# Cross attention with values by query and one row of 32 rounds; window attention's head in four transfers

## The chip, the cores and the metric

The kernel runs on one core of a Trainium2 chip. The metric is device time in microseconds (us) of one execution, taken as the median of several runs. The engines are TensorE (PE; its weight loads are PEld), VectorE (DVE), ScalarE (ACT), GpSimd (POOL) and SyncE (SP), which issues all transfers here. TensorE's clock is granted at one of two levels, 1.2 and 2.4 GHz; the profile gives the mean of a stretch as a share of 2.4 GHz.

## The reference

Two decoder layers, written as six stages on x (4 sequences, 512 tokens, 512 features). The change touches two: the attention with a window of layer 1, and its cross attention, which is, in float32:

```
q = rms(x @ Wq) * gq     # 16 heads of 128, 512 queries
k = rms(ctx @ Wk) * gk ; v = ctx @ Wv      # ctx: 512 x 256
e = exp(q @ k.T / sqrt(128))
o = (e @ v) / sum(e over the keys)
x = layernorm(x + concat(o) @ Wo)
```

## The kernel before, in words

The stages run one after the other, with a barrier between them. In each, five programs (one per engine) meet through semaphores. PSUM is 8 banks of 128x512 float32; a table gives each result a bank, and PE waits (`wait_empty`) until the last result of that bank has been read. Products with the weights and the scores are made of three products of float32r halves (`split3`, lines 198 to 200: high x high, high x low, low x high). Transposes and products with the probabilities are plain float32, and each such product is two records in the profile.

**Cross attention** (`cross_attention`, L1633) treats two heads at a time: 8 rounds for each of 4 sequences, 32 in all. A round computes the attention of heads y and, interleaved, the projections of the heads x of the next round. `turns` (L1731) puts this into loops: for each sequence a loop of seven rounds, and then a round that is preceded by `start` (the next sequence's x is turned: 16 transposes on PE from a copy `x_cur`, halves by ACT and DVE) and followed by `finish` (the normalisation, on DVE). On PE a round is: scores of both heads (24 products 128x512); `values(0)`, four products with v as weights and the probabilities (keys by queries) moving, 512 columns; `queries(0)`; `sums(0)`, one product of ones with the probabilities summed by POOL over the key tiles; `values(1)`, `sums(1)`; `queries(1)`; four `keys_values`; `project_out(0)`; the transposes of k and q (L2014); `project_out(1..3)`. The values lie as features by queries, so DVE inverts a whole 128x512 tile of sums (L1925), multiplies (L1928) and hands it to ACT and DVE for the halves (L1874, L1932). Projections and transposes use three banks in turn, scores and outputs three, the values one each. The low halves of the new weights are made by POOL in one piece of 2048 columns and one of 1024 (L1792).

**Window attention** (`window_attention`, L1167) begins by loading the weights of the projection in one transfer of 1536 KB (L1304). ACT takes the high half of all of it in one instruction (L1366), POOL and DVE take the low half, two k blocks each (L1329, L1452). PE waits first for a chain of memsets on POOL (L1543), turns x, and then waits for all low halves (L1571) before the first projection. After it, a row for the bias is added (L1559).

The quoted core of the values before:

```
mm = pe.matmul(pb.ap(("o", h)), v[:, k, h * DX:(h + 1) * DX], probsT[:, h, k, :],
               start=(k == 0), stop=(k == T - 1))
```

Of the kernel before, what the change touches and what calls it, by code (L numbers as in the profile page):

```python
# [20 lines left out]
P = 128  # L21
B, S, D = 4, 512, 512
# [9 lines left out]
DX = 128  # L32
# [1134 lines left out]
def window_attention(c):  # L1167
# [12 lines left out]
    with ExitStack() as ctx:  # L1180
# [42 lines left out]
        weights, small = c.sem("s4_weights_loaded"), c.sem("s4_small_loaded")  # L1223
        bias_in, wo_in = c.sem("s4_bias_loaded"), c.sem("s4_wo_loaded")
        w_hi, w_lo_pool, w_lo_dve = c.sem("s4_w_hi_ready"), c.sem("s4_w_lo_first_half"), c.sem("s4_w_lo_second_half")
# [77 lines left out]
        def _(sp):  # L1303
            sp.dma_start(w[:, :, :], d["l1a_wqkvT"].rearrange("(k p) n -> p k n", p=P)).then_inc(weights, 16)  # L1304
# [14 lines left out]
        def _(pool):  # L1319
# [4 lines left out]
            pool.memset(ones[SB:SB + 1, :].bitcast(F32), 1.0)  # L1324
            pool.drain()
            pool.memset(kT[STK:P, :, :].bitcast(F32), 0.0).then_inc(zeros_set, 1)
            pool.drain()
            pool.wait_ge(w_hi, 1)
            pool.tensor_tensor(w_l[:, 0:2, :], w[:, 0:2, :], w_h[:, 0:2, :].bitcast(F32), ALU.subtract).then_inc(w_lo_pool, 1)  # L1329
# [28 lines left out]
        def _(act):  # L1358
# [6 lines left out]
            act.wait_ge(weights, 16)  # L1365
# [3 lines left out]
            act.activation(bias[0:1, :], braw[0:1, :], ACT.Copy)  # L1369
            act.activation(bias[SB:SB + 1, :], braw[SB:SB + 1, :], ACT.Copy).then_inc(bias_hi, 1)  # L1370
            act.wait_ge(small, 16 * 5)
            act.activation(idb[:, :], c.ident[:, :], ACT.Copy)
            act.activation(mask[:, :], maskf, ACT.Copy).then_inc(bf_ready, 1)
            act.wait_ge(tables, 1)
            act.wait_ge(q_frame, 1)

            for ph, b, *s in seq:
                if ph == "X" and b > 0:
                    turned_hi(b, s[0])
                elif ph == "Pq":  # L1380
                    t = s[0]
                    act.wait_ge(*ps.full(0, ("Pq", b, t)))
# [44 lines left out]
                elif ph == "e":  # L1427
                    h = s[0]
                    act.wait_ge(*ps.full(0, ("e", b, h)))
                    if h % 4 == 0 and b * NH + h >= NPB:  # L1430
                        act.wait_ge(*ps.full(0, ("o", *divmod((b * NH + h - NPB) // 4, NKV), 1)))
# [10 lines left out]
        def _(dve):  # L1442
# [8 lines left out]
            dve.wait_ge(w_hi, 1)  # L1451
            dve.tensor_tensor(w_l[:, 2:KD, :], w[:, 2:KD, :], w_h[:, 2:KD, :].bitcast(F32), ALU.subtract).then_inc(w_lo_dve, 1)  # L1452
# [26 lines left out]
            dve.wait_ge(bf_ready, 1)  # L1479
# [62 lines left out]
        def _(pe):  # L1542
            pe.wait_ge(zeros_set, 1)  # L1543

# [6 lines left out]
            def projected(key, b, t, lo, hi):  # L1551
                out = ps.ap(key)[:, 0:hi - lo]
                ps.wait_empty(pe, 0, key)
                for k in range(KD):
                    split3(pe, out, (c.xhi[:, k, t * P:(t + 1) * P], c.xlo[:, k, t * P:(t + 1) * P]),
                           (w_h[:, k, lo:hi], w_l[:, k, lo:hi]), k == 0, False)
                if b == 0 and t == 0:
                    pe.wait_ge(bias_lo, 1)
# [1106 lines left out]
```

## Time and profile before

| what | value |
|---|---|
| median of 3 runs | 2571.3 us (2570.89 to 2572.88) |
| the profiled execution | 2571.21 us, its span 2569.4 us |
| PE busy over the span | 2187.9 us (85%) |
| DVE, ACT, POOL busy | 1408.9, 1207.9, 909.8 us |
| window attention | about 777 to 1165 us of the span |
| cross attention | about 1165 to 2300 us |
| a transfer of 512 KB of wq, issue to landing | 4.6 us (median of 33) |
| the transfer of 1536 KB of window weights | 6.4 us |
| `RECIPROCAL` of the sums, 128x512 | 64 of 3.356 us on DVE |

The profile is one execution of the program. Its timeline gives for each instruction, or row of equal ones, the start, the duration, the engine, the line, what is written and read, and in square brackets the idle time of that engine before it and who ended it. Matmuls are pipelined: the start of one to the start of the next is the rate, the duration is longer.

### The profile page before, as it was taken

The page shows a single profiled execution, that of the slowest core. Times are in us where ns is not written, and L with a number is a line of the kernel's source. Part 1 is how long each engine was busy: PE and PEld are TensorE (multiplying, and loading weights), DVE is VectorE, ACT ScalarE, POOL GpSimd, SP SyncE. Part 2 cuts the span into 40 slices and gives each one's busy share as a digit, 9 for nine tenths or more (in the row PEclk, how much of TensorE's full clock was granted, in tenths as well). Part 3 has the DMA queues.
Part 4 walks back from the last instruction along what each step waited for, and adds up shares of the span by engine and source line. Part 5 has one row for each costly group of instructions (what it writes and reads, how often), then busy time and mean ns, then how long its engine had stood idle before and what let it go on. Part 6 is the DMA issues. An engine that isn't in the chain of part 4 may idle for free. (4 is left out here: it accounts for less than half of the span.)

```text
span 2569.4 us, 36165 instructions
## 1 busy us (share of the span) xinstructions
PE 2187.9 (85%) x12664; PEld 1555.7 (61%) x12664; DVE 1408.9 (55%) x2138; ACT 1207.9 (47%) x2272; POOL 909.8 (35%) x569
## 2 busy tenths in 40 slices
PE   5989989867895787795999999999999999967772
PEld 4555646446774665554777767777777677744340
DVE  4656666644545435542555665557556755552637
ACT  3636464534324635534555545554555555531513
POOL 3525242410003202203455455555555555530101
PEclk9999999988897999997999999999999999988886
DMA  2000000010001000003111211121111111111001
GB/s 109 1 1 1 1 1 1 1 62 1 1 1 48 1 1 1 1 1 117 36 38 49 74 49 49 49 73 33 41 49 49 49 49 49 49 37 69 1 1 65
DMA packets 62367, 84.15 MB, mean 33 GB/s; under 512 B 6132, under 2 KB 41332, under 8 KB 61752
## 3 DMA queue, kind: packets, MB, share of 16 engines
q1 hardware_dynamic: 62264, 82.76, 9.5%
q8 instruction: 67, 1.10, 0.2%
q14 instruction: 36, 0.29, 0.0%
HBM read 74.36 MB, written 4.19 MB: 31 GB/s over the span
## 5 line engine op out<-in xcount | busy, mean ns | idle before, releaser
L1925 DVE RECIPROCAL s_inv_sums<-banks 128x512 f32<-128x512 f32 x64 | 214.8, 3356 | 343.3 <-PE banks L2038 340.0
L1799 POOL TENSOR_TENSOR s_qk_rstd<-s_mean_sq,minus_half 128x8 f32<-128x8 f32 x64 | 118.7, 1854 | 502.0 <-DVE s_mean_sq L1912 502.0
L2031 PE MATMUL banks<-s_probsT,s_v 128*128 128x512 f32 x512 | 231.2, 594 | 0.0
L1862 ACT ACTIVATE s_probsT<-banks,s_minus_bound,s_qk_rstd 128x512 f32<-128x512 f32 x256 | 177.0, 782 | 92.5 <-PE banks L200 88.5
L594 DVE TENSOR_REDUCE s_neg_max<-banks 128x1 f32<-128x512 f32 x256 | 165.4, 684 | 87.9 <-PE banks L660 86.3
L543 ACT ACTIVATE s_probsT<-banks 128x512 f32<-128x512 f32 x256 | 148.7, 600 | 81.5 <-PE banks L674 79.1
L1833 ACT ACTIVATE s_squares<-banks 128x512 f32<-128x512 f32 x64 | 38.2, 597 | 288.0 <-PE banks L200 287.9
L198 PE MATMUL banks<-s_w_proj_hi,xT_hi 128*128 (+1 forms) x512 | 170.8, 334 | 2.9 <-DVE s_ctxT_lo L1973 2.9
L2031 PEld LDWEIGHTS banks<-s_probsT,s_v 128*128 128x128 f32 x512 | 97.6, 191 | 111.1 <-issue 108.5
L1792 POOL TENSOR_TENSOR s_w_proj_lo<-s_w_proj_raw,s_w_proj_hi 128x2048 f32 (+1 forms) x33 | 152.0, 4607 | 14.0 <-ACT s_w_proj_hi L1825 14.0
L1808 POOL TENSOR_TENSOR s_probs_pair_sums<-s_probsT 128x1024 f32<-128x1024 f32 x64 | 151.0, 2360 | 7.2 <-issue 7.2
L199 PE MATMUL banks<-s_w_proj_lo,xT_hi 128*128 (+1 forms) x512 | 145.7, 285 | 0.0
L200 PE MATMUL banks<-s_w_proj_hi,xT_lo 128*128 (+1 forms) x512 | 145.6, 284 | 0.0
L482 POOL TENSOR_TENSOR x_cur<-s_probsT 128x512 f32<-128x512 f32 x64 | 82.1, 1283 | 156.6 <-PE banks L692 109.9
L660 PE MATMUL banks<-s_kT,s_qT 128*128 128x512 f32 x256 | 117.8, 464 | 7.0 <-ACT s_qT L532 3.3
L198 PE MATMUL banks<-s_wqkv_hi,xT_hi 128*128 128x512 f32 (+1 forms) x256 | 92.0, 360 | 34.6 <-POOL s_wqkv_lo L464 8.8
L674 PE MATMUL banks<-s_qT,s_kT 128*128 128x512 f32 x256 | 106.3, 415 | 16.2 <-ACT s_qT L536 14.0
L198 PEld LDWEIGHTS banks<-s_w_proj_hi,xT_hi 128*128 128x128 f32 x512 | 98.9, 193 | 18.1 <-issue 18.1
L198 PE MATMUL banks<-s_w_out_hi,s_outT_hi 128*128 (+1 forms) x256 | 104.4, 408 | 5.8 <-DVE s_outT_lo L1932 5.8
L199 PEld LDWEIGHTS banks<-s_w_proj_lo,xT_hi 128*128 128x128 f32 x512 | 99.0, 193 | 14.8 <-issue 14.8
L198 PE MATMUL banks<-s_w_proj_hi,s_ctxT_hi 128*128 (+1 forms) x256 | 101.2, 395 | 6.9 <-ACT s_v L1848 6.9
L1958 DVE TENSOR_TENSOR x_all<-banks,x_all 128x512 f32 (+1 forms) x128 | 85.5, 688 | 38.1 <-PE banks L200 35.0
(409 smaller groups left out, 5896.4 us busy)
## 6 DMA issues: line engine op xcount, KB each, us to landing
s_w_proj_raw<-l1x_wq SPq DMA_DIRECT2D x33, 512.0 KB, 4.6
s_w_out_raw<-l1x_wo SPq DMA_DIRECT2D x33, 512.0 KB, 3.6
s_w_proj_raw<-l1x_wk SPq DMA_DIRECT2D x33, 256.0 KB, 4.8
s_w_proj_raw<-l1x_wv SPq DMA_DIRECT2D x33, 256.0 KB, 5.1
x_all<-x SPq DMA_DIRECT2D x4, 1024.0 KB, 12.3
s_ctxT<-ctxT SPq DMA_DIRECT2D x8, 512.0 KB, 5.7
x_cur<-x_all SPq DMA_DIRECT2D x4, 1024.0 KB, 7.7
out<-x_all SPq DMA_DIRECT2D x4, 1024.0 KB, 4.3
```

The lines of the kernel that those rows point to most:

```text
L198: pe.matmul(out, lhs[0], rhs[0], start=start, stop=False)
L199: pe.matmul(out, lhs[0], rhs[1], start=False, stop=False)
L200: return pe.matmul(out, lhs[1], rhs[0], start=False, stop=stop)
L543: act.activation(probsT[:, h % NPB, k, :], ps.ap(s), ACT.Exp).then_inc(ps.freed(s), 1)
L594: dve.tensor_reduce(nmax[:, h % 2, t, 0:1], ps.ap(s), AX.X, ALU.max, negate=True) \
L660: pe.matmul(ps.ap(s), qT[:, h % NQB, t * P:(t + 1) * P], kT[:, h % NKV, :], start=True, stop=True).then_inc(ps.filled(s), 1)
L1792: pool.tensor_tensor(out, raw, hi.bitcast(F32), ALU.subtract).then_inc(done.sem, 1)
L1799: pool.tensor_tensor(rs[:, j, :, :], ms[:, j, :, :], c.mhalf[:, 0:T * HP].rearrange("p (t h) -> p t h", h=HP), ALU.pow) \
L1808: pool.tensor_tensor(psum2[:, :, :], probsT[:, h, 0:2, :], probsT[:, h, 2:4, :], ALU.add)
L1862: act.activation(probsT[:, h, k, :], pb.ap(("e", h, k)), ACT.Exp, bias=bound[:, 0:1], scale=rs[:, 1, k, h:h + 1]).then_inc(pb.freed(("e", ...
L1925: dve.reciprocal(inv[:, h, :], pb.ap(("sum", h))).then_inc(pb.freed(("sum", h)), 1)
L2031: mm = pe.matmul(pb.ap(("o", h)), v[:, k, h * DX:(h + 1) * DX], probsT[:, h, k, :], start=(k == 0), stop=(k == T - 1))
```

## The change

In the window attention: the weights come in four transfers, ACT takes the high half block by block, POOL takes one block of the low half (k = 1) and DVE three, PE waits block by block within the first projection, and it no longer waits for the memsets at the start. The clearing of `kT` moves behind POOL's block.

In the cross attention: the loops are gone, and one list `seq` sets the order of all engines for 32 rounds. x is turned straight from `x_all`, two rounds ahead. The values now have the probabilities as weights (128x128) and v with a column of ones moving (129 columns): 16 products of 129 columns for each head, which give queries by features, with the sum in column 128. DVE inverts two sums per partition and multiplies (`M`), and PE turns the result (`OT`, 4 transposes for each head) one round later. POOL's sums, `sums` and the 128x512 reciprocals are gone. The halves of the weights are made apart for q and for k and v. Projections and transposes have two banks instead of three, the values two for each head (5 and 6) shared by both heads, `OT` one. The normalisation is made of pieces: statistics on DVE behind each output tile, the last step on ACT.

The diff, cut to its core:

```diff
-            sp.dma_start(w[:, :, :], d["l1a_wqkvT"].rearrange("(k p) n -> p k n", p=P)).then_inc(weights, 16)
+            for k in range(KD):
+                sp.dma_start(w[:, k, :], d["l1a_wqkvT"].rearrange("(k p) n -> p k n", p=P)[:, k, :]).then_inc(weights[k], 16)
...
-            pool.tensor_tensor(w_l[:, 0:2, :], w[:, 0:2, :], w_h[:, 0:2, :].bitcast(F32), ALU.subtract).then_inc(w_lo_pool, 1)
+            pool.wait_ge(w_hi, 2)
+            pool.tensor_tensor(w_l[:, 1, :], w[:, 1, :], w_h[:, 1, :].bitcast(F32), ALU.subtract).then_inc(w_lo_pool, 1)
...
-            act.activation(w_h[:, :, :], w[:, :, :], ACT.Copy).then_inc(w_hi, 1)
+            for k in range(KD):
+                act.wait_ge(weights[k], 16)
+                act.activation(w_h[:, k, :], w[:, k, :], ACT.Copy).then_inc(w_hi, 1)
...
-            pe.wait_ge(zeros_set, 1)
...
+                    if b == 0 and t == 0 and lo == 0:
+                        pe.wait_ge(*((w_lo_pool, 1) if k == 1 else (w_lo_dve, {0: 1, 2: 2, 3: 3}[k])))
...
+        for j in range(-1, N + 1):
+            now, nxt, prv, border = 0 <= j < N, j + 1 < N, 0 <= j - 1, (j + 2) % G == 0 and j + 2 < N
+            if now:
+                seq += [("E", j, 0, k) for k in range(T)]
+            if prv:
+                seq.append(("OT", j - 1, 0))
+            if nxt:
+                seq.append(("Q", j + 1, 0))
+            if prv:
+                seq.append(("OT", j - 1, 1))
+            if now:
+                seq += [("E", j, 1, k) for k in range(T)] + [("V", j, 0)]
+            if j + 2 < N:
+                seq.append(("WQ", j + 2))
...
+                seq += [("Q", j + 1, 1), ("MQ", j + 1)]
+            if now:
+                seq.append(("M", j, 0))
...
+            if border:
+                seq += [("X", (j + 2) // G, k) for k in range(KD)]
...
+            if prv:
+                seq.append(("O", j - 1, 0))
+            if nxt:
+                seq.append(("NQ", j + 1))
+            if now:
+                seq.append(("V", j, 1))
+            if nxt:
+                seq.append(("KV", j + 1, 0))
+            if now:
+                seq.append(("M", j, 1))
+            if nxt:
+                seq += [("KV", j + 1, 1), ("TQ", j + 1, 0), ("KV", j + 1, 2)]
...
+                seq += [("TQ", j + 1, 1), ("KV", j + 1, 3), ("MK", j + 1)]
...
+            if s[0] in ("Q", "KV", "TK", "TQ") or s[0] == "X" and s[2] % 2:
+                uses.append((s, na % 2, 1))
+                na += 1
+            elif s[0] in ("E", "O", "X"):
+                uses.append((s, 2 + nb % 3, 1))
+                nb += 1
+            elif s[0] == "V":
+                uses += [((*s, u), 5 + u, 1) for u in range(2)]
+            elif s[0] == "OT":
+                uses.append((s, 7, 1))
...
+                    for u in range(2):
+                        key, tt = ("V", j, h, u), slice(2 * u, 2 * u + 2)
+                        dve.wait_ge(*ps.full(0, key))
+                        out = ps.ap(key)[:, 0:2 * (DX + 1)].rearrange("p (t n) -> p t n", t=2)
+                        dve.reciprocal(inv[:, h, tt], out[:, :, DX])
+                        dve.drain()
+                        dve.tensor_tensor(o[:, h, tt, :], out[:, :, 0:DX], inv[:, h, tt].unsqueeze(2).broadcast_to([P, 2, DX]),
+                                          ALU.mult).then_inc(ps.freed(key), 1)
...
+                                mm = pe.matmul(ps.ap(key)[:, t * (DX + 1):(t + 1) * (DX + 1)], probs[:, h, k, q_tile],
+                                               v[:, k, h, :], start=(k == 0), stop=(k == T - 1))
```

`E` are scores, `Q` and `KV` projections, `TQ` and `TK` transposes, `V` values, `M` quotients, `OT` their transposes, `O` outputs, `MQ` and `MK` mean squares, `NQ` the normalised q.

On DVE, in the middle of a round of the cross attention, there stood before (the two reciprocals of the sums, then the mean squares of the next q, then the low halves of the outputs):

```order
L1925 RECIPROCAL s_inv_sums<-banks 128x512
...
L1928 TENSOR_TENSOR s_inv_sums<-banks,s_inv_sums 128x512
...
L1909 TENSOR_REDUCE s_mean_sq<-s_squares 128x8
L1912 TENSOR_SCALAR s_mean_sq<-s_mean_sq 128x8
...
L1932 TENSOR_TENSOR s_outT_lo<-s_inv_sums,s_outT_hi 128x512
...
L1919 TENSOR_TENSOR s_q<-s_q,s_qk_rstd 128x1024
```

And now, at the same place (`x_cur` holds the squares now; the first two rows are `MQ`, the next four `M` of head 0):

```order
L1948 TENSOR_REDUCE s_mean_sq<-x_cur 128x8
L1951 TENSOR_SCALAR s_mean_sq<-s_mean_sq 128x8
L1997 RECIPROCAL s_inv_sums<-banks 128x2
L1999 TENSOR_TENSOR s_out_by_query<-banks,s_inv_sums 128x256
...
L2010 TENSOR_TENSOR x_all<-banks,x_all 128x512
L1977 TENSOR_TENSOR s_q<-s_q,s_qk_rstd 128x1024
```

The mean squares stood behind the first head's quotients and now stand ahead of them; the first output tile stands between the quotients and the normalised q.

On PE, in the part from the last query projection to the second transposes of q, there stood before (`...` stands for further products of the same kind):

```order
L2038 MATMUL banks<-s_probs_sum,ones_sb 128x512
...
L198 MATMUL banks<-s_w_proj_hi,xT_hi 128x256
...
L198 MATMUL banks<-s_w_proj_hi,s_ctxT_hi 128x512
...
L198 MATMUL banks<-s_w_out_hi,s_outT_hi 128x512
...
L2014 MATMUL banks<-ident_sb,s_k 128x128 x4
```

And now:

```order
L198 MATMUL banks<-s_w_proj_hi,xT_hi 128x256
...
L198 MATMUL banks<-s_w_out_hi,s_outT_hi 128x512
...
L2096 MATMUL banks<-s_v_and_ones,s_probsT 128x129 x16
L198 MATMUL banks<-s_w_proj_hi,s_ctxT_hi 128x512
...
L2030 MATMUL banks<-ident_sb,s_q 128x128 x4
L198 MATMUL banks<-s_w_proj_hi,s_ctxT_hi 128x512
```

The second head's values moved from ahead of the queries to behind them and behind one output tile, and the transposes of q moved in between the projections of keys and values.

## Rows read from the trace of the kernel before

**Rows 1.** Busy time by engine, stretch of cross attention (PE, PEld, DVE, ACT, POOL, granted clock).

```profile
1165.00:2293.00 1128.00, 1071.45 (x5056) 804.50 (x5056) 646.20 (x670) 576.00 (x1048) 583.68 (x261) 0.98 0.15 52
```

**Rows 2.** Timeline of PE, one round: start, duration, engine, line, operation, [idle before].

```profile
1312.21 3.60 PE L2031 MATMUL banks<-s_probsT,s_v 128*128 128x512 f32 x8
...
1315.76 0.28 PE L199 MATMUL banks<-s_w_proj_lo,xT_hi 128*128 x1
...
1318.52 1.02 PE L2038 MATMUL banks<-s_probs_sum,ones_sb 128*128 128x512 f32 x2
...
1319.37 3.60 PE L2031 MATMUL banks<-s_probsT,s_v 128*128 128x512 f32 x8
...
1326.53 0.39 PE L198 MATMUL banks<-s_w_proj_hi,s_ctxT_hi 128*128 x1
...
1333.50 1.03 PE L2014 MATMUL banks<-ident_sb,s_k 128*128 128x128 f32 x8
...
1336.24 0.39 PE L199 MATMUL banks<-s_w_out_lo,s_outT_hi 128*128 x1
...
1345.56 1.88 PE L2031 MATMUL banks<-s_probsT,s_v 128*128 128x512 f32 x4
```

**Rows 3.** Timeline of ACT in the same round.

```profile
1326.73 0.60 ACT L1833 ACTIVATE s_squares<-banks 128x512 f32<-128x512 f32 x1 [3.18 <-PE banks L200]
...
1332.31 0.38 ACT L1844 ACTIVATE s_squares<-banks 128x256 f32<-128x256 f32 x1 [0.29 <-PE banks L200]
...
1332.85 0.39 ACT L1848 ACTIVATE s_v<-banks 128x256 f32<-128x256 f32 x1
```

**Rows 4.** DVE: timeline of the same round; groups by line (busy, mean ns).

```profile
1327.86 1.21 DVE L1909 TENSOR_REDUCE s_mean_sq<-s_squares 128x8 f32<-128x1024 f32 x1
...
1329.29 1.30 DVE L1932 TENSOR_TENSOR s_outT_lo<-s_inv_sums,s_outT_hi 128x512 fp32r<-128x512 f32 x2
...
L1019 DVE RECIPROCAL s_sim_inv_sums<-s_sim_sums 128x1 f32<-128x1 f32 x16 | 1.6, 149 | 0.5 <-ACT s_probs L945 0.5
...
L1520 DVE TENSOR_TENSOR x_cur<-banks,s_inv_sums 128x128 f32<-128x128 f32 x64 | 18.7, 292 | 4.8
```

**Rows 5.** Timeline of PE in the last stage: float32 products of 128 columns.

```profile
2354.17 3.84 PE L2531 MATMUL banks<-s_kkT_by_head,s_wq 128*128 128x128 f32 x32 [0.95 <-DVE s_kkT_by_head L2342]
...
2365.00 3.74 PE L2472 MATMUL banks<-s_slotsT,s_wv 128*128 128x128 f32 x32
```

**Rows 6.** Timeline at the borders of the cross attention: SP, then PE.

```profile
1166.12 0.33 SPq L1749 DMA_DIRECT2D s_gains<-l1x_gq  x1
...
1185.22 0.55 PE L198 MATMUL banks<-s_w_proj_hi,xT_hi 128*128 128x256 f32 x1 [2.94 <-DVE s_ctxT_lo L1973]
...
1212.16 3.59 PE L2031 MATMUL banks<-s_probsT,s_v 128*128 128x512 f32 x8
...
2266.76 3.60 PE L2031 MATMUL banks<-s_probsT,s_v 128*128 128x512 f32 x8
...
2300.68 1.73 PE L2484 MATMUL banks<-ident_sb,x_all 128*128 128x128 f32 x7 [7.35 <-PEq L1646]
```

**Rows 7.** PE timeline; then busy time and granted clock of three stretches.

```profile
1503.76 0.50 PE L198 MATMUL banks<-s_w_proj_hi,s_ctxT_hi 128*128 x1 [2.29 <-ACT s_v L1848]
...
1500.00:1510.00 10.00, 7.39 (x31) 5.47 (x29) 6.28 (x9) 5.31 (x16) 2.08 (x1) 0.83 0.00 0
...
1775.00:1785.00 10.00, 7.17 (x39) 5.63 (x38) 7.65 (x12) 6.70 (x18) 2.08 (x1) 1.00 0.00 0
...
2268.00:2278.00 10.00, 7.64 (x15) 3.06 (x14) 3.38 (x2) 0.00 (x0) 8.03 (x5) 0.83 0.14 52
```

**Rows 8.** Timeline of the window attention's head: POOL, PE.

```profile
788.36 4.99 POOL L1329 TENSOR_TENSOR s_wqkv_lo<-s_probsT,s_wqkv_hi 128x1536 fp32r<-128x1536 f32 x1 [6.95 <-ACT s_wqkv_hi L1366]
...
793.71 0.77 PE L198 MATMUL banks<-s_wqkv_hi,xT_hi 128*128 128x512 f32 x1 [8.72 <-POOL s_wqkv_lo L1329]
...
798.69 0.39 PE L1559 MATMUL banks<-s_bias_rows,s_ones_rows 128*128 128x512 f32 x1
```

More of the change, by code:

```diff
@@ L1364, in _ @@
                 turned_hi(0, k)
-            act.wait_ge(weights, 16)
-            act.activation(w_h[:, :, :], w[:, :, :], ACT.Copy).then_inc(w_hi, 1)
+            for k in range(KD):
+                act.wait_ge(weights[k], 16)
+                act.activation(w_h[:, k, :], w[:, k, :], ACT.Copy).then_inc(w_hi, 1)
             act.wait_ge(bias_in, 16 * 4)
             act.wait_ge(zeros_set, 1)
[L1369 to L1374, printed above, removed]
+            for row in (SB, 0):
+                act.activation(bias[row:row + 1, :], braw[row:row + 1, :], ACT.Copy).then_inc(bias_hi, 1)
             act.wait_ge(q_frame, 1)
@@ new lines, in cross_attention @@
+        seq.append(("LX", B - 1))
+        uses, na, nb = [], 0, 0
+        for s in seq:
+            if s[0] in ("Q", "KV", "TK", "TQ") or s[0] == "X" and s[2] % 2:
[8 more added lines that the diff above has]
+                uses.append((s, 7, 1))
@@ L1889, in start @@
-            def start(b):
-                c.act_x_hi(act, b, (b, b * G), pa)
-                act.wait_ge(*ctx_in.after(b, 16))
-                act.activation(c_h[:, :, :], cT[:, :, :], ACT.Copy).then_inc(ctx_hi.sem, 1)
-            turns(act, start, body, nothing)
+                        sqr.then_inc(squared["k"].sem, 1)
+                    act.activation(kk[:, t, :], kv[:, 0:NW], ACT.Copy)
+                    if j > 0 and t == 0:
+                        act.wait_ge(*ps.full(0, ("V", j - 1, 1, 1)))
@@ new lines, in _ @@
+            for ph, j, *s in seq:
+                key = (ph, j, *s)
+                if ph == "X":
+                    turned(key, lambda t: c.x[:, j * T + t, s[0] * P:(s[0] + 1) * P])
+                elif ph == "Q":
+                    i = s[0]
+                    if i == 0:
+                        pe.wait_ge(*wq_lo.after(j, 1))
+                        if j % G == 0:
+                            for k in range(KD):
+                                pe.wait_ge(*ps.released(0, ("X", j // G, k)))
+                    ps.wait_empty(pe, 0, key)
@@ L2052, in body @@
-                if x is not None:
-                    queries(0)
-                if y is not None:
-                    sums(0)
-                    values(1)
-                    sums(1)
-                if x is not None:
-                    queries(1)
-                    for t in range(T):
-                        keys_values(t)
-                if y is not None:
-                    pe.wait_ge(*wo_lo.after(y, 1))
-                    for h in range(HP):
-                        pe.wait_ge(*pb.released(y, ("o", h)))
-                    project_out(0)
@@ L2068, in body @@
-                if x is not None:
-                    transposed("kT", kk, pa.released(x, ("kv", T - 1)))
-                    transposed("qT", q, q_normed.after(x[1], 1))
-                if y is not None:
-                    for t in range(1, T):
-                        project_out(t)
-            def start(b):
-                c.pe_turn_x(pe, b, (b, b * G), pa)
-            turns(pe, start, body, nothing)
-        pa.close(B * G, B)
-        pb.close(B * G)
-        c.close_common()
+                                        (side(wx_h, j)[:, w], side(wx_l, j)[:, w]), k == 0, k == KD - 1)
```

628 lines of the change are left out of this document (331 added, 297 removed).

## Prediction

> **What bounds the kernel now.** I read the busy times by stretch first. In the cross attention PE is busy 1071 of 1128 us, the granted clock 0.98 of 2.4 GHz [rows 1]; DVE, ACT and POOL each do about half. So PE sets the time here, and the reciprocals of 3.36 us on DVE and the sums on POOL, which the change removes, lie beside PE's work. What is to be priced is PE's own work and its waits. Then I read one round in PE's timeline [rows 2]: the values of head 0 start at 1312.21 and again at 1345.56, a round is 33.35 us. In it PE waits once, about 0.5 us, at the transposes. From the first values to those of the last round are 31 rounds, 1212.16 to 2266.76 [rows 6], 1054.6 us. At 33.35 they would be 1033.9: 20.7 us are extra, at the three changes of sequence and behind them (one is the wait of 2.29 us in [rows 7]).
>
> **Values.** Before: 1312.21 to 1315.64 (0.12, one product of 256 columns, ahead of the second one at 1315.76), 3.43 us a head; the sums take 1318.52 to 1319.37, 0.85 [rows 2]. Both heads: 8.56. Now each head has 16 products of 129 columns, 32 records. The nearest row is a chain of 16 float32 products of 128 columns, each with weights of its own: 32 records in 3.74 us, the last one lasting about 0.28, so 0.112 each [rows 5]. Ends: 0.112, and 0.118 from the other row (3.84 us, with a slow first one). I take 0.112, whose operands are alike in form: 3.6 us a head, 7.2 both (7.6 at 0.118).
>
> **Transposes.** Before: 1333.50 to 1336.01 (0.23 ahead of 1336.24), 2.51 with the wait, for 16 [rows 2]. Now 24, in six groups of four, each between float32r products. Eight in a row take 0.87; a group of four and the way back to float32r about 0.50, against 0.44 from that rate alone. I take 0.50: 3.0 in all (2.6 at the lower end). The other products, 33.35 - 8.56 - 2.51 = 22.3, stay as they are. Work of a round: 22.3 + 7.2 + 3.0 = 32.5.
>
> **First new wait: the second head's values.** On PE the order is the second query projection, one output tile (6 products of 0.23, 1.38 us), then the values of head 1. These need bank 5, which held the first head's values and is freed by the quotient `M` on DVE. But `M` stands on DVE behind the mean squares `MQ` of the projection that PE has just ended. The chain from the end of the projection: 0.20 until ACT starts (1326.53 to 1326.73), 0.60 for the squares [rows 2, 3]; 0.03; 1.43 from the start of the reduction to the next instruction of DVE (1327.86 to 1329.29) [rows 4]; a reciprocal of two columns, 0.15 by the row of one column; 0.08; the product of 128x256, between 0.29 (128x128) and twice that, I take 0.43; 0.1 to PE. Sum 3.0. PE has 1.4 us of other work. It waits 1.6, and 0.1 is lost at the restart: **1.7 us** in each round. Queued behind this wait on PE are the values, keys, transposes and three outputs, nothing passes it.
>
> **Second new wait: the third keys and values.** Projections and transposes have two banks now. `KV` 2 uses the bank of `KV` 1, which ACT frees after three instructions: 0.20, then 1332.31 to 1333.24 [rows 3], and 0.06, together 1.19. Between them PE has one group of transposes, 0.50. Wait 0.7, restart 0.1: **0.8 us**. The other bank pairs have more work in between (the first score of the next round, behind the transposes of k, by 0.2 us only).
>
> So a round is 32.5 + 1.7 + 0.8 = **35.0 us**, 1.65 more than before.
>
> **The 31 rounds.** 31 x 35.0 = 1085.0. The turning of x (16 transposes, 2.0 us) lies ahead of the wait of 1.7 and fills it; I add 0.4 for each of three, and 0.6 for the statistics in front of the transposed k one round behind: 3.0. The first round has no outputs and no turned values, 2.1 less; the last has no queries in front, 1.2 less. 1084.7 against 1054.6: **+30.1**. The extras of before go with that: the wait for late mean squares at the changes, and the copy of x.
>
> **Head of the stage.** Before, the transfers start at 1166.12, the queries at 1185.22 and the first values at 1212.16 [rows 6]. Now the 512 KB of wq go first (4.6 us), ACT and DVE make the halves (1.05 and 1.23 for 1024 columns), x needs no copy: queries at about 1173.5, 11.7 earlier. In the first lap there is nothing to cover the normalised q (a chain of 5.6 us against two `KV` of 1.4): 3 us of wait, with a fall of the clock 1.7 more, and 1 at the transposes of k; on the other side the wait of 2.5 us for the scores goes. I take the first values at 1205.4: **-6.8** (-4 to -9).
>
> **Tail.** Before, 33.9 us from the last round's values to the next stage [rows 6], of which 26.6 to PE's end. Now values, an output, values, three outputs, 12.8; two groups of transposes, 1.0; a wait for ACT and DVE behind each group, 1.6 each (three products of the first output lie in the second); the other 21 of the 24 products, 4.9; end at 21.9, and the 7.3 behind it as before: 29.2. **-4.7** (-3 to -7).
>
> **Head of the window attention.** Before, POOL's half takes 4.99 us and PE waits 8.72 for it; the first projection runs 793.71 to 798.69 [rows 8]. Now the first block is ready when the turned x is (PE starts 3.7 us earlier, without the memsets), about 783.8; POOL's block is half as large, 2.5, at 786.1; the last at about 786.5; the projection ends at about 790.2. The bias row (on DVE, behind its blocks) is ready about then. **-8.5** (-5 to -10): what follows is a chain through ACT, DVE and POOL that starts with this projection, so the whole gain is kept.
>
> **Sum.** +30.1 - 6.8 - 4.7 - 8.5 = +10.1. The profiled execution took 2571.2, the median is 2571.3: 2581.3 us.
>
> **Rivals.** (1) *The round is shorter than summed*, the place is the wait in front of the second head's values. It decides at 34.5 us a round: below that the kernel is faster by 0.2%. For it: my prices of 0.50 for a group of transposes (at 0.44 a round loses 0.4) and of two restarts (0.2) are rounded up; if DVE's chain were 2.6 instead of 3.0, 0.4 more. All three: 34.0, 31 us less, 2550. If the first wait were wholly covered, 33.3 and 2529. Against it: each link has a row, and the order on DVE leaves `M` behind `MQ`.
>
> (2) *The clock.* A wait of 2.29 us was followed by a stretch at 0.83 of 2.4 GHz over 10 us, 3.4 us at the level of 1.2 GHz, which costs 1.7; the same wait 275 us later was followed by 1.00; one of 2.35 us at the end again by 0.83 [rows 7]. Waits of 0.5 us never did it. The new wait is 1.6, with one of 0.7 some 7 us behind. If a third of 31 rounds lost 1.7: +18, 2599; if all: +53, 2634. The Trainium skill (TensorE: Matmul & The Clock Gate, section HAM oscillation) states that a loop which waits in each iteration can pay the fall of the clock in every one of them; by that rule it would be the last figure. In this trace a wait of 1.6 us in a row of dense work has no twin, so I leave this a rival.
>
> (3) *The 129-column passes show their weight loads.* A load of 128x128 float32 is recorded with 0.19 us. If a pass took that, 64 of them would be 12.2 instead of 7.2: +155, 2736. Against it stands the row of 0.112 with the same loads [rows 5]. At 0.118 it is only +12, 2593, which is in my range.
>
> (4) *The change doesn't do what it says*, for example the transfers in four parts land no sooner than the one: then -8.5 becomes about -4, 2586.
>
> **How the numbers follow.** A measurement of this kernel can tell about 0.2% (5 us) from no change. Chances: forecast with its own spread (0.3 us a round either way), 2571 to 2591: 0.48; rival 1: 0.28; rival 2: 0.16; rival 3 in full: 0.02; the small cases of 3 and 4: 0.06. The bounds of the terms that add over the rounds (0.112 to 0.118, 0.44 to 0.50, waits of 2.0 to 2.5) give 2560 to 2595; with the clock in a third of the rounds up to 2605, and half of rival 1 down to 2553. Range 2553 to 2605. Faster 0.28, same 0.22, slower 0.50.
>
> **What would show it.** In the profile of the changed kernel: the round, from one head 0's values to the next, at 35.0; PE's waits for DVE's quotient ahead of the second head's values, 31 times about 1.6; and for ACT's copy of v, about 0.7; passes of 0.112; the first queries at 7 us behind the stage's first transfer; the window projection some 8 us earlier. It is wrong if the round is under 34.5, which would mean a wait that I put on PE isn't there, or if the granted clock of the stage falls below 0.95.

## The result, and the profile after

The changed kernel takes 2582.4 us (median of 6 runs, 2581.4 to 2584.1), the kernel before in the same series 2571.0 us: a ratio of 1.0043, interval 1.0032 to 1.0053, or 11.4 us slower. The prediction was 2581.3, slower. The profiled execution has a span of 2579.6 us.

One round in PE's timeline, after (columns as in [rows 2]):

```profile
1305.40 3.73 PE L2096 MATMUL banks<-s_v_and_ones,s_probsT 128*128 128x129 f32 x32
...
1311.84 0.40 PE L198 MATMUL banks<-s_w_out_hi,s_outT_hi 128*128 128x512 f32 x1
...
1314.80 3.84 PE L2096 MATMUL banks<-s_v_and_ones,s_probsT 128*128 128x129 f32 x32 [1.39 <-DVE s_out_by_query L1999]
1318.39 0.48 PE L198 MATMUL banks<-s_w_proj_hi,s_ctxT_hi 128*128 128x512 f32 x1
...
1321.26 0.60 PE L2030 MATMUL banks<-ident_sb,s_q 128*128 128x128 f32 x4
...
1322.44 0.50 PE L198 MATMUL banks<-s_w_proj_hi,s_ctxT_hi 128*128 128x512 f32 x1 [0.59 <-ACT s_v_and_ones L1906]
...
1340.20 3.73 PE L2096 MATMUL banks<-s_v_and_ones,s_probsT 128*128 128x129 f32 x32
```

The round is 34.80 us (1305.40 to 1340.20; 33.35 in [rows 2]). Both waits that were forecast stand where they were put. PE's groups of instructions between 1225 and 2285 give their number: 1.39 us in front of the second head's values adds up to 37.9 us, 0.59 in front of the third keys and values to 16.8 (columns: busy time, mean ns of one, idle time ahead and what ended most of it):

```profile
L2096 PE MATMUL banks<-s_v_and_ones,s_probsT 128*128 128x129 f32 x1950 | 230.4, 276 | 37.9 <-DVE s_out_by_query L1999 37.9
L198 PE MATMUL banks<-s_w_proj_hi,s_ctxT_hi 128*128 128x512 f32 x240 | 102.9, 429 | 16.8 <-ACT s_v_and_ones L1906 16.8
```

The stretch of the cross attention (columns as in [rows 1]), where the granted clock is 0.99 against 0.98 before, and DVE has 508 us of work for 646:

```profile
1160.00:2304.00 1144.00, 1068.19 (x6715) 931.36 (x6713) 508.43 (x794) 585.00 (x1088) 357.33 (x162) 0.99 0.15 47
```

The chain behind the wait, DVE's timeline after: reduction, its scaling, and only then the quotients.

```profile
1312.67 1.22 DVE L1948 TENSOR_REDUCE s_mean_sq<-x_cur 128x8 f32<-128x1024 f32 x1 [8.08 <-ACT x_cur L1889]
1313.97 0.17 DVE L1951 TENSOR_SCALAR s_mean_sq<-s_mean_sq 128x8 f32<-128x8 f32 x1
1314.07 0.17 DVE L1997 RECIPROCAL s_inv_sums<-banks 128x2 f32<-128x2 f32 x1
1314.32 0.42 DVE L1999 TENSOR_TENSOR s_out_by_query<-banks,s_inv_sums 128x256 f32<-128x256 f32 x1
...
1315.89 3.36 DVE L1977 TENSOR_TENSOR s_q<-s_q,s_qk_rstd 128x1024 f32<-128x1024 f32 x1
```

DVE had sat idle for 8.08 us before it; the values of head 0 had been in their bank since 1308.9. PE waits for an engine that is free, and that takes the two jobs in the wrong order.

Where the 10 us of span went, by places that both traces have:

| stretch | before | after | difference | forecast |
|---|---|---|---|---|
| start of the window attention (first transfer) to start of the cross attention | 388.5 | 380.7 | -7.8 | -8.5 |
| start of the cross attention to its first values | 46.0 | 40.1 | -6.0 | -6.8 |
| first values to those of round 31 | 1054.6 | 1083.1 | +28.5 | +30.1 |
| from there to the next stage's first product | 33.9 | 28.8 | -5.1 | -4.7 |
| sum | | | +9.6 | +10.1 |

### The profile page after: what moved, and what is told of

The parts are those of the page before. It is cut to its first block and busy times, and to the rows that moved or that the text cites. A ratio compares the mean times of both kernels' runs of the same rounds, so it can differ in the third digit from the quotient of the medians.

```text
span 2579.6 us, 36278 instructions
## 1 busy us (share of the span) xinstructions
PE 2183.9 (85%) x14293; PEld 1683.6 (65%) x14328; DVE 1266.9 (49%) x2257; ACT 1221.2 (47%) x2321; POOL 680.2 (26%) x471
## 5 line engine op out<-in xcount | busy, mean ns | idle before, releaser
L2096 PE MATMUL banks<-s_v_and_ones,s_probsT 128*128 128x129 f32 x2048 | 243.5, 277 | 40.6 <-DVE s_out_by_query L1999 40.6
L2096 PEld LDWEIGHTS banks<-s_v_and_ones,s_probsT 128*128 128x128 f32 x2048 | 237.9, 192 | 55.9 <-DVE s_out_by_query L1999 52.6
L1948 DVE TENSOR_REDUCE s_mean_sq<-x_cur 128x8 f32<-128x1024 f32 x64 | 78.1, 1220 | 255.8 <-ACT x_cur L1889 244.8
L198 PE MATMUL banks<-s_w_proj_hi,xT_hi 128*128 128x256 f32 x512 | 150.9, 295 | 2.9 <-DVE s_w_proj_lo L1971 2.9
L199 PE MATMUL banks<-s_w_proj_lo,xT_hi 128*128 128x256 f32 x512 | 145.6, 284 | 0.0
L200 PE MATMUL banks<-s_w_proj_hi,xT_lo 128*128 128x256 f32 x512 | 145.5, 284 | 0.0
L198 PE MATMUL banks<-s_w_proj_hi,s_ctxT_hi 128*128 128x512 f32 x256 | 110.3, 431 | 18.6 <-ACT s_v_and_ones L1906 18.6
L2010 DVE TENSOR_TENSOR x_all<-banks,x_all 128x512 f32<-128x512 f32 x128 | 87.9, 687 | 60.0 <-PE banks L200 58.0
L198 PE MATMUL banks<-s_qkT_hi 128*128 128x512 f32 x256 | 108.9, 425 | 2.8 <-DVE s_qkT_lo L1987 2.8
L1853 POOL TENSOR_TENSOR s_w_out_lo<-s_w_out_raw,s_w_out_hi 128x1024 fp32r<-128x1024 f32 x32 | 103.2, 3227 | 10.2 <-ACT s_w_out_hi L1883 10.2
```

The costliest lines, as they stand in the source:

```text
L198: pe.matmul(out, lhs[0], rhs[0], start=start, stop=False)
L199: pe.matmul(out, lhs[0], rhs[1], start=False, stop=False)
L200: return pe.matmul(out, lhs[1], rhs[0], start=False, stop=stop)
L1853: pool.tensor_tensor(side(wo_l, j), raw_o[:, :], side(wo_h, j).bitcast(F32), ALU.subtract) \
L2010: dve.tensor_tensor(xt, ps.ap(("O", j, t)), xt, ALU.add).then_inc(ps.freed(("O", j, t)), 1)
L2096: mm = pe.matmul(ps.ap(key)[:, t * (DX + 1):(t + 1) * (DX + 1)], probs[:, h, k, q_tile], v[:, k, h, :], start=(k == 0), stop=(k == T - 1))
```

## Experiments

Each edit is against the changed kernel, unless it says otherwise.

**One step moved: the quotient ahead of the mean squares.**

```
-                seq += [("Q", j + 1, 1), ("MQ", j + 1)]
+                seq.append(("Q", j + 1, 1))
             if now:
                 seq.append(("M", j, 0))
+            if nxt:
+                seq.append(("MQ", j + 1))
```

> The changed kernel with one step moved: the quotient of head 0 stands ahead of the mean squares of q in the order of every engine. Theory (PE pays for DVE's order): the quotient needs only the values, which PE has ended 1.4 us before the projection ends, so it is written before PE comes to the second head's values; the wait of 1.39 us (27 times, 37.9 us in the trace) goes with its restart: the round falls from 34.81 to 33.4, the time from 2582.4 to about 2542 (2538 to 2548), faster than the kernel before. Rival A (the wait only moves: the mean squares, now 1.2 us later, hold back the normalised q and PE waits in front of the transposes of q instead): the round stays at 34.3 or more, 2567 or more. Rival B (the clock had also paid for the waits): the round falls by more than 1.6 us, below 2532.

Measured: 2530.0 us, ratio to before 0.9836 (0.9820 to 0.9852), 52.4 us less than the changed kernel. The wait is gone without another in its place, and the round is 33.16 (1303.61 to 1336.77): 1.65 less. The theory holds for the cause, but the time lies below its range of 2538 to 2548, and by the bound that was written down (2532) rival B, the clock, would win. In the steady rounds it doesn't: the granted clock there was 1.00 before the edit too. It has a part in one place, the stage's first round, where two falls of the clock are gone with the wait, 3.3 of the 52 us (see the first round below). For the rest, what was short is the price of a wait. PE's idle time is counted from a modelled end. The last product ahead of this wait is recorded with 0.39 to 0.40 us, while its successor usually comes after 0.23, so some 0.16 us of waiting do not show as idle; and the values of head 1 take 3.59 us to the next product behind the wait, 3.49 without it, 0.1 more. So this wait costs PE the recorded time and 0.26 us: 1.39 + 0.26 = 1.65.

**One bank changed: the transposed q to bank 7.**

```
-            if s[0] in ("Q", "KV", "TK", "TQ") or s[0] == "X" and s[2] % 2:
+            if s[0] == "TQ":
+                uses.append((s, 7, 1))
+            elif s[0] in ("Q", "KV", "TK") or s[0] == "X" and s[2] % 2:
```

> The changed kernel with the transposed q written to bank 7, where only the turned values are written, so that the third keys and values take the bank of the first and not of the second. Theory: the wait of 0.59 us for ACT's copy of v (30 times, 16.9 us) goes with a restart of 0.1: the round falls from 34.81 to 34.15, the time to about 2562 (2559 to 2567). Rival (another wait for ACT comes due at the next product, since ACT is what is late and not the bank): less than 6 us gained, 2577 or more.

Measured: 2553.4 us, 0.9928 (0.9911 to 0.9944), 29 us less. PE's timeline with this edit:

```profile
1335.65 3.73 PE L2098 MATMUL banks<-s_v_and_ones,s_probsT 128*128 128x129 f32 x32
1345.05 3.84 PE L2098 MATMUL banks<-s_v_and_ones,s_probsT 128*128 128x129 f32 x32 [1.39 <-DVE s_out_by_query L2001]
...
1369.61 2.62 PE L2098 MATMUL banks<-s_v_and_ones,s_probsT 128*128 128x129 f32 x22
```

That is under the 2559 to 2567 that was expected, again for the price of the wait. The first wait stays at 1.39, the round is 33.96: 0.85 less, again 0.59 + 0.26. The 0.26 is made up differently here: the four transposes ahead of this wait are recorded with 0.60 us where the next product otherwise comes after 0.35, and the product behind it takes 0.34 for 0.32. 31 rounds of it are 26 us; the first lap of the stage gives 0.9 and a fall of the clock less in the first round 1.6.

**Both edits.**

> Both edits at once, so that PE has neither new wait. Theory: they add up: the round is the work alone, 32.8 us, and the time about 2522 (2516 to 2530), 49 us under the kernel before. Rival A (the work of the new form is more than summed and the waits only covered it, for example by ACT or DVE which stay behind): a round of 33.4 or more, 2540 or more. Rival B (with fewer waits the clock gives something back): under 2512.

Measured: 2506.2 us, 0.9743 (0.9726 to 0.9759), 65 us under the kernel before. In a round the two add up (1.65 + 0.85 = 2.50 against 2.51): the round is 32.30, 0.2 under the 32.5 of work in the prediction. In the total they don't quite (52.4 + 29.0 = 81.4 against 76.2). Of these 5.2 us, 2.0 are in the first round, where either edit alone takes away the same fall of the clock, and 1.5 are a new fall behind the last round; the rest is no more than what single executions differ by. The expectation of 2522 counted neither the price of the restarts, 0.52 us a round or 16 us, nor the falls of the clock in the first round; its rival B, the clock, explains no more than those 3.3 us. In a steady round no wait of PE is recorded any more.

**The window attention of the kernel before.**

> The changed kernel with the window attention of the kernel before, in full; the cross attention stays as changed. Theory: the head of the window attention gave 9.4 us in the trace (bias product at 789.6 for 798.7, less 0.3 that the stage began later), and all of it reached the end: 2591.5 (2589.5 to 2593.5), 20.5 over the kernel before. Rival (the stage behind swallows part of the gain at its chain through ACT, DVE and POOL, and the cross stage's head gave the rest): under 2588.

Measured: 2588.9 us (2585.8 to 2590.8), 6.6 us over the changed kernel. Medians alone leave this between the two expectations, since one execution differs from another by some 2 us even ahead of the place that differs: the stage's first transfer starts at 780.32 here and at 776.27 in another run. The stage's own length is sharper. From its first transfer to that of the cross attention it takes 388.3 us here, 388.5 in the kernel before and 380.7 in the changed one. The seven other runs with the new head and four transfers lie between 380.8 and 381.0, so the change is worth 7.3 to 7.8 us there, not 9.4. The timeline of ACT in the changed kernel shows what gave 1.7 of it back:

```profile
793.08 1.28 ACT L1403 ACT_TABLE_LOAD   x1
794.37 0.22 ACT L1403 ACTIVATE s_rms<-s_mean_sq 128x20 f32<-128x20 f32 x1
794.49 0.29 ACT L1384 ACTIVATE s_ident_bf<-ident_sb 128x128 bf16<-128x128 f32 x1
794.70 0.62 ACT L1385 ACTIVATE s_mask<-s_probsT 128x512 bf16<-128x512 f32 x1
```

The copies of the identity and the mask (0.8 us here) stood in ACT's idle time ahead of the first projection in the kernel before, and now they stand between the root and the next squares. That they are a part of what was given back is read from their place, and was not tried by itself.

**The kernel before, with the second transposes of q behind the second output tile.**

```
-                    transposed("qT", q, q_normed.after(x[1], 1))
+                    transposed("qT", q, q_normed.after(x[1], 1), (0,))
                 if y is not None:
-                    for t in range(1, T):
+                    project_out(1)
+                if x is not None:
+                    transposed("qT", q, q_normed.after(x[1], 1), (1,))
+                if y is not None:
+                    for t in range(2, T):
```

> The kernel before with one step of PE moved: the transposes of q for head 1 stand behind the second output tile, so that PE no longer waits 0.54 us for DVE in front of them. The other runs have shown that a wait costs PE what is recorded and 0.26 us more. Theory: the round falls by 0.8, from 33.35 to 32.55, and the time by 25 us, to about 2547 (2543 to 2551). The round without waits is then 32.55 with the sums in matmuls and 32.30 with the column of ones: the new form is worth 0.25 us a round, and the rest of the 65 us between this kernel and the one of the third run comes from the heads, the tail and the changes of sequence. Rival (the wait of before was in truth larger or smaller work of another kind, and the column of ones itself is what saves): this kernel gains under 12 us, 2560 or more.

Measured: 2585.3 us, 1.0053 (1.0036 to 1.0070): 14 us slower, where 25 faster were expected. The wait at the transposes went, and another came. PE's timeline, the scores behind the outputs:

```profile
1345.94 0.50 PE L198 MATMUL banks<-s_qkT_hi 128*128 128x512 f32 x1 [0.87 <-DVE x_all L1958]
```

The second score needs the bank of output tile 1, and DVE adds that tile only after q's second head and the mean squares of k. Moving the transposes on PE moved all that stands behind them on DVE. The round is 33.79.

**The same with DVE's order changed as well** (against the run above):

```
-                    transposed_lo("qT", 1)
+                    transposed_lo("qT", 1, (0,))
                     mean_squares(1, "k")
                 if y is not None:
-                    for t in range(1, T):
+                    add_out(1)
+                if x is not None:
+                    transposed_lo("qT", 1, (1,))
+                if y is not None:
+                    for t in range(2, T):
```

> The kernel of the fifth run with DVE's order changed too: its mean squares of k and the addition of the second output tile stand ahead of the lower half of q's second head. In the fifth run PE waited 0.86 us in front of the scores for a bank that this addition frees, and the round was 33.79. Theory: that wait goes, the round is the work of the old form, 32.55 and 0.1 for the second group of transposes, 32.65: 31 times 0.7 less than before, 2550 (2546 to 2554). The column of ones then has 0.25 to 0.35 us a round to its credit, and most of the 65 us of the third run come from elsewhere. Rival (the old form keeps PE waiting somewhere whatever the order, because DVE with its two reciprocals of 3.36 us is late in each round): 2565 or more, and the column of ones is worth what it frees on DVE.

Measured: 2555.5 us, 0.9931 (0.9914 to 0.9948). The round is 32.79 (1309.85 to 1342.64), without a recorded wait; 0.14 over the forecast, of which 0.1 is a product of a score that takes 0.50 where the others take 0.39. So the old form can be had almost without waits too, and what the column of ones saves on PE is worth 32.79 - 32.30 = 0.5 us a round, 15 us in 31. The remaining 34 us to the 2506.2 are the changes of sequence and the stage's first and last round (22 us beyond 31 rounds in this kernel, 5.5 in the other), the window attention (7.6), the stage's head (5.9) and tail (3.5). Some 5 of the 22 us are the clock: at all three changes PE waits 2.27 to 2.30 us for ACT's copy of v, and the granted clock is 0.83 in the 10 us around each.

**The reduction of the squares twice: a longer wait.**

> The changed kernel with the reduction of the squares of q done twice (1.22 us more on DVE, ahead of the first head's quotient; the result is the same). Theory: PE pays one for one: its wait for the quotient grows from 1.39 to about 2.7, in 28 to 31 rounds, with the clock at 1.00 as before: 38 to 42 us, 2622 (2618 to 2627). Rival (a wait of more than 2 us brings the clock down behind it, as two of four did in the kernel before): 1.7 us more in each round that it takes: 2640 if a third, 2675 if all.

Measured: 2663.6 us, 1.0361. The rival won, and nearly in full. PE's timeline and the granted clock (last but two of a row's numbers) in the 10 us that follow, and in the 18 behind those:

```profile
1325.56 4.70 PE L2097 MATMUL banks<-s_v_and_ones,s_probsT 128*128 128x129 f32 x25 [2.68 <-DVE s_out_by_query L2000]
```

```profile
1321.00:1331.00 10.00, 7.32 (x43) 6.70 (x43) 8.08 (x11) 2.97 (x4) 6.02 (x3) 0.83 0.22 67
1331.00:1349.00 18.00, 17.41 (x97) 14.55 (x96) 7.52 (x12) 9.47 (x21) 2.89 (x2) 1.00 0.13 46
```

The wait is 2.68 for 1.39, as forecast, but the round is 37.75 (1314.87 to 1352.62): 1.29 more for the wait and 1.65 more for a stretch at 1.2 GHz. 0.83 over 10 us is 3.4 us at half clock, the same as in [rows 7]. Two of the 28 rounds with a wait of 2.68 or more kept their clock and took 36.1, which is 34.81 and 1.29 and nothing else. In the others the second head's values take 5.2 to 5.5 us for 3.84; in a single one (at 1248.78) they take 6.78, and that round is 2.9 longer than one without a fall.

**Half the reduction twice: a wait of about two microseconds.**

> The changed kernel with the reduction over half of q's squares done once more (about 0.7 us on DVE, same result), half of what the sixth run added. There a wait of 2.68 us was followed by values that took 6.78 us instead of 3.73 and a clock of 0.83 over 10 us, in each round, so that 1.29 us more of wait cost 2.94. Theory A (the cost is proportional to the wait beyond some length): about 1.5 us a round, 2625. Theory B (a step: either the clock falls in full or not at all): if it doesn't fall, 0.7 us a round, 2603 (2600 to 2606), the values at 3.8; if it does, 2.35 a round, 2650.

The 6.78 us that this expectation starts from were those of one round, and not of each; the 2.94 are right all the same, as 1.29 for the wait and 1.65 for the clock.

Measured: 2647.5 us, 1.0286. Theory B, the step, with the clock falling. PE's timeline, two rounds of it:

```profile
1249.14 3.84 PE L2099 MATMUL banks<-s_v_and_ones,s_probsT 128*128 128x129 f32 x32 [2.15 <-DVE s_out_by_query L2002]
1274.58 3.73 PE L2099 MATMUL banks<-s_v_and_ones,s_probsT 128*128 128x129 f32 x32
1284.73 5.48 PE L2099 MATMUL banks<-s_v_and_ones,s_probsT 128*128 128x129 f32 x32 [2.15 <-DVE s_out_by_query L2002]
```

```profile
1249.00:1255.00 6.00, 5.86 (x42) 5.45 (x43) 5.53 (x9) 0.58 (x3) 6.00 (x3) 1.00 0.24 74
1285.00:1291.00 6.00, 6.00 (x37) 5.82 (x37) 5.28 (x7) 0.00 (x0) 6.00 (x3) 0.72 0.26 86
```

Of the 28 waits of 2.15 us or more two were followed by values of 3.84 us and the other 26 by values of 5.48, 1.64 more; the granted clock in the two stretches shown, one of each kind, is 1.00 and 0.72. A round of the second kind is 37.24 (1311.78 to 1349.02): 34.81 + 0.76 + 1.65. In the changed kernel none of the 26 waits of 1.39 was followed by a fall, and one of 1.72 was not either:

```profile
2047.93 3.84 PE L2096 MATMUL banks<-s_v_and_ones,s_probsT 128*128 128x129 f32 x32 [1.72 <-DVE s_out_by_query L1999]
```

So in a round like this the falls set in somewhere between 1.72 us, where the one wait brought none, and 2.15. The Trainium skill (TensorE: Matmul & The Clock Gate, section HAM oscillation) says that a loop with a wait in each iteration can pay for the clock each time; these two kernels agree, the changed kernel shows that not every wait does it. The page's own loop waits longer in each iteration than the 2.15 us of this run.

**One transfer for the window attention's weights.**

```
-            for k in range(KD):
-                sp.dma_start(w[:, k, :], ...[:, k, :]).then_inc(weights[k], 16)
+            sp.dma_start(w[:, :, :], ...).then_inc(weights[0], 16)
```

> The changed kernel with the window attention's projection weights in one transfer again; the halves are still made block by block by ACT, DVE and POOL. Theory: the one transfer lands 6.4 us after its issue, at about 784.3 of the trace, where now the blocks land from one to the other up to 785.0; ACT's four copies (0.78 each) then end at 787.5 for 785.9, the last product of the first projection comes 1.6 us later, and the time is 2584 (2583 to 2585.5). So the four transfers are worth 1.6 of the 7.8 us that the window attention gives, and the smaller block on POOL and the way there the rest. Rival (the four transfers are what brought it): 2588 or more.

Measured: 2580.7 us (2579.5 to 2582.1), 1.0038 (1.0024 to 1.0052): no loss in the time. The stage's length is 381.5 for 380.7 to 381.0 in the kernels with four, so at most 0.8 us. ACT's timeline shows why, first with four transfers, then with one:

```profile
782.04 1.56 ACT L1370 ACTIVATE s_wqkv_hi<-s_probsT 128x768 fp32r<-128x768 f32 x2
784.10 0.85 ACT L1370 ACTIVATE s_wqkv_hi<-s_probsT 128x768 fp32r<-128x768 f32 x1 [0.49 <-DMA s_probsT<-l1a_wqkvT]
785.10 0.84 ACT L1370 ACTIVATE s_wqkv_hi<-s_probsT 128x768 fp32r<-128x768 f32 x1 [0.15 <-DMA s_probsT<-l1a_wqkvT]
```

```profile
782.60 3.04 ACT L1369 ACTIVATE s_wqkv_hi<-s_probsT 128x768 fp32r<-128x768 f32 x4 [2.01 <-DMA s_probsT<-l1a_wqkvT]
```

The transfers are issued at 777.94 and 776.27. The whole lands after 6.3 us, the last of four parts after 7.1. ACT ends its copies 8.0 us behind the issue with four and 9.4 with one; the start of the chain behind (ACT's first square, 790.34 and 790.65) is 2.0 apart, and of that 1.2 is lost again before the stage ends. Part of it lies in PE's keys just behind: with four transfers the granted clock is 0.50 from 785.6 to 791.4, and their first products are recorded with 0.41 us; with one it is 0.50 from 784.5 to 790.1, ahead of the keys, and they take 0.28. So at least 6.8 of the 7.6 us of the window attention come from the rest of the edit. Two parts can be read from the traces, but were not tried one by one: POOL's subtraction of 1.86 us for 4.99, and PE that no longer waits for the memset (3.8 us, 10.54 against 6.77 of idle time at the stage's start).

**POOL's two halves behind its roots of k** (against the run with both edits: `WKl` and `WOl` stand behind `MK`).

> The kernel of the third run with POOL's two halves (k and v weights, output weights) placed behind its reciprocal roots of k, so that nothing runs on POOL while DVE normalises q. Theory: DVE's normalisation of 128x1024 takes 3.36 us because POOL works at the same time; alone it takes 1.23. In the steady rounds nobody waits for it; in the first lap PE's wait at the transposes of q (4.5 us) falls by about 2. Time 2504 for 2506 (2503 to 2506), the row of the normalisation at 1.2 to 1.3. Rival A (the 3.36 us are the work's own at its new place): it stays at 3.3 and the time at 2506. Rival B (the halves now come late, and PE waits for the weights at the next keys and values): over 2510.

Measured: 2500.3 us, 0.9722 (0.9706 to 0.9738), 6 us less than with both edits, 3 more than forecast. DVE's normalisation of q in a round:

```profile
1300.88 1.23 DVE L1981 TENSOR_TENSOR s_q<-s_q,s_qk_rstd 128x1024 f32<-128x1024 f32 x1 [1.16 <-POOL s_qk_rstd L1842]
```

and POOL's halves, here while DVE works in PSUM, and in the changed kernel:

```profile
1313.43 2.40 POOL L1853 TENSOR_TENSOR s_w_proj_lo<-s_w_proj_raw,s_w_proj_hi 128x1024 fp32r<-128x1024 f32 x1
1315.79 2.39 POOL L1857 TENSOR_TENSOR s_w_out_lo<-s_w_out_raw,s_w_out_hi 128x1024 fp32r<-128x1024 f32 x1
```

```profile
1315.82 2.35 POOL L1849 TENSOR_TENSOR s_w_proj_lo<-s_w_proj_raw,s_w_proj_hi 128x1024 fp32r<-128x1024 f32 x1
1318.12 3.39 POOL L1853 TENSOR_TENSOR s_w_out_lo<-s_w_out_raw,s_w_out_hi 128x1024 fp32r<-128x1024 f32 x1
```

1.23 us for 3.36: the long time was the company of POOL. The rows of the changed kernel show how. POOL's first half began at 1315.82, 0.07 ahead of DVE's normalisation, and took its usual 2.35 us, as if alone. DVE's operation ended 1.08 behind POOL's end, and POOL's second half, which began while DVE's operation was still open, is the one that took 3.39 for 2.39. In the first lap it is the same: POOL 1177.36 to 1179.70, DVE 1177.42 to 1180.77. So the two look as if they took turns, whole operation by whole operation; no run tries the other order. In the steady rounds nobody waits for it; in the first lap PE's wait at the transposes of q falls from 4.52 to 2.39, in the second the waits of 0.99 and 0.16 become one of 0.55, and the first values start 36.0 us into the stage, for 39.2. These are some 4 us; the rest of the 6 is within what single executions differ by ahead of the stage, and wasn't traced further.

**The two ends of the stage** (against the run above: `KV` 2 ahead of `TQ` 0 in the first lap, the turned head 1 of the last two rounds in bank 0).

> The kernel of the eighth run with two edits at the ends of the stage: in the first lap the third keys and values stand ahead of the transposes of q, and in the last two rounds the turned values of head 1 go to bank 0 and not to bank 7. Theory: PE's wait in the first lap falls from 2.39 to about 1.0, the waits of 1.78 and 1.50 at the tail fall to 0.3 or less: 4 us in all, 2496 (2494 to 2499). Rival (the end of the stage hangs on ACT and DVE turning the two heads, not on the bank): 1.5 us or less, 2499 or more.

Measured: 2498.2 us, 0.9709 (0.9692 to 0.9725), 2.1 less. Half of it failed: the first values start 36.05 us into the stage, as before; the wait of 2.39 has become 0.45 for ACT, 0.30 for the normalised q and 1.56 for bank 7. The tail gave what was forecast: no wait in front of the turned head 1, the round before the last 29.3 us for 31.3, and 27.4 us from the last round's values to the next stage for 28.8. These are 3.4 us where the medians show 2.1, which is within what single executions differ by. This kernel is 2.9% faster than the one before.

## Why the prediction was right

**The rounds.** Forecast 35.0, measured 34.81 (34.80 from 1305.40 to 1340.20; 31 rounds take 1083.1 with the extras). The two waits were forecast at 1.7 and 0.8 with their restarts, and cost 1.65 and 0.85 by the runs that took them away. The way there was a little off: 1.6 was forecast as recorded and 1.39 is, and the cost of a restart is 0.26, not 0.1. The two errors cancel for the first wait, which is luck. DVE's chain from the end of the projection to the quotient is the sum of rows that was written down, 3.0 us.

**The work.** Forecast 32.5, measured 32.30 without waits. The values take 3.49 us and 0.09 on the way back, 3.6 as forecast (0.109 a product; weight loads are recorded with 192 ns and lie beside them, so rival 3 is out). The transposes were mis-sized: a group of four and the way back takes 0.35 + 0.09 = 0.44, the lower end of the two that were given, 2.6 a round and not 3.0. The rest of the work is 22.5 for 22.3.

**Rival 1** needed a round under 34.5 and did not get it. Its last case, the first wait wholly covered, was priced at 33.3 a round and 2529; the first experiment covers it, with 33.16 and 2530.

**Rival 2, the clock.** It did not happen at 1.39 us, and happened in nearly every round at 2.15. In the changed kernel's rounds it happened in the first alone, and there twice (below). The forecast rested on "a wait of 1.6 us in a row of dense work has no twin" and gave 0.16; what wasn't seen is how near the edge was: 0.76 us more on DVE cost 65 us, 24 for the wait and the rest for the clock.

**The first round and the changes of sequence.** Forecast 3.0 more and 3.3 less than 31 equal rounds, together -0.3; measured 1083.1 - 31 x 34.81 = +4.0. The changes of sequence gave 2.6 for 3.0, and the waits vanish at them, as forecast; the last round gave 1.0 less for 1.2. The first round failed: "the first round has no outputs and no turned values, 2.1 less", but it took 37.10 (1198.66 to 1235.76), 2.3 more. The missing output tile is the one that covers the wait; without its 1.38 us the wait is 2.76, and the clock fell behind it. It fell once more at the end of the same round, behind waits of 0.59, 0.59, 1.03 and 0.98 us in a row. PE's timeline, and the granted clock in both places:

```profile
1208.02 5.20 PE L2096 MATMUL banks<-s_v_and_ones,s_probsT 128*128 128x129 f32 x30 [2.76 <-DVE s_out_by_query L1999]
```

```profile
1206.00:1216.00 10.00, 7.98 (x44) 7.42 (x45) 6.77 (x11) 3.20 (x6) 7.27 (x3) 0.83 0.21 58
```

```profile
1222.65 1.09 PE L2030 MATMUL banks<-ident_sb,s_k 128*128 128x128 f32 x8 [1.03 <-ACT s_v_and_ones L1906]
1224.72 0.57 PE L198 MATMUL banks<-s_qkT_hi 128*128 128x512 f32 x1 [0.98 <-DVE s_qkT_lo L1987]
1225.08 0.63 PE L199 MATMUL banks<-s_qkT_lo,s_qkT_hi 128*128 128x512 f32 x1
```

```profile
1222.00:1230.00 8.00, 6.38 (x28) 5.18 (x29) 2.68 (x4) 4.57 (x9) 1.64 (x1) 0.79 0.01 2
```

With the quotient ahead of the mean squares the same round is 31.25 (1198.21 to 1229.46), 1.9 less than its neighbours, as the prediction had it. Of the 5.85 between the two, 2.76 + 0.26 + 1.65 = 4.7 are this wait and the fall behind it, and 1.6 the second fall; the other waits of the round are 0.4 shorter on balance. So the step of the prediction that failed here is that it took the missing output tile as work saved only, and not as cover lost. The round's 0.19 x 31 = 5.9 on the other side hid this error of 4.3. That the forecast of the whole came within 1.1 us of the measured time is luck in this sense: single terms are off by 4 to 6 us and cancel. The sign and the two waits are not.

**Head, tail and window attention.** The head gave 6.0 for 6.8: PE waits 4.5 us at the transposes of q in the first lap, forecast 3, because the normalisation takes 3.35 us beside POOL and not 1.23; in the trace of before it never took more than 1.23. The tail gave 5.1 for 4.7. In the window attention the first projection comes 9.4 us earlier and the stage 7.8: the step that failed is "so the whole gain is kept"; and the landing in four parts, for which rival 4 allowed some 4.5 us, is worth under 1.

## What to carry to other kernels

When an engine that holds back the busiest one is itself idle for microseconds, look at the order of its own queue first: one step moved gave 52 us, a bank 29, and the change in the arithmetic around which all was built 15. In a round like this one, price a recorded wait between matmuls with 0.26 us on top (two waits were taken away to show it), and take a wait that grows past 1.7 us in each round as something that may nearly double its price at once. Where work is taken away, ask what wait it had covered: the first round lost one output tile and became 2.3 us longer. And when a step of one engine is moved, walk down the others' queues behind it, as the run that was 14 us slower shows.

## What the runs showed of the hardware

- Repeated waits of PE of 1.39 us in dense work, and one of 1.72, never brought the granted clock down; waits of 2.15 to 4.05 did in all but four of 56, mostly at 1.3 to 1.7 us each and once at 2.9. Four waits of 0.59 to 1.03 us within 8 us, shortly behind such a fall, were followed by another one.
- A DVE operation of two SBUF operands, 128x1024, takes 1.23 us alone and 3.36 when a POOL subtraction of the same size started just ahead of it, which itself keeps its 2.35; the POOL subtraction that starts while DVE's is still open takes 3.39 for 2.39. The DVE operations on PSUM that ran beside POOL's halves stayed at 0.69.
- A load of 1536 KB in one transfer landed 6.3 us after its issue; in four, the last landed about 7.1 behind the first issue.
